# Products of keys and queries for the transposed scores as 64-row tiles, two banks at a time

## The reference, cut to what matters

```python
B, T, D, S, H = 32, 112, 256, 375, 16            # DH = 16
def xattn(k, q):                                 # k = context (B, S, D), q = layernorm(x) (B, T, D)
    qh, kh, vh = heads(q @ wq + bq), heads(k @ wk + bk), heads(k @ wv + bv)
    logits = einsum('bhqd,bhkd->bhqk', qh, kh) / sqrt(16) + mask * -1e9
    return einsum('bhqk,bhkd->bhqd', softmax(logits), vh) @ wo + bo
x = x + xattn(ctx, layernorm(x))
x = x + moe_ffn(layernorm(x))                    # top-1 of 8 experts, 1024 hidden units
```

## Time and profile before

| | us |
|---|---|
| median of 3 runs | 864.75 |
| lowest, highest | 863.34, 866.98 |
| profiled execution, its own time | 873.9 |
| its span, first to last instruction | 872.2 |

### The profile page before, as it was taken

How to read it: one execution, slowest core, us unless ns; L and a number is a source line. 1 busy time by engine, 2 the same in 40 slices (tenths; PEclk the granted TensorE clock), 3 DMA queues, 4 the chain that set the end, 5 groups by cost and what they waited for, 6 DMA issues and landing times.

```text
span 872.2 us, 27918 instructions
## 1 busy us (share of the span) xinstructions
PE 781.0 (90%) x8480; PEld 554.7 (64%) x8480; DVE 565.9 (65%) x1823; ACT 435.5 (50%) x1032; POOL 523.5 (60%) x753
## 2 busy tenths in 40 slices
PE   5799999999999999999999999981698988987894
PEld 4466666666666666666666666550577867776683
DVE  4667777777777777777777777638354545554352
ACT  3266666666666666666666666540323323322231
POOL 5676677677766777777677677561535435445311
PEclk9899999999999999999999999995799999999798
DMA  5776577667766876788678767605312222222110
GB/s 164 201 182 187 162 199 202 184 170 198 208 166 181 198 218 182 205 211 226 167 209 217 209 186 191 176 13 214 109 47 80 65 62 80 63 66 86 39 31 8
DMA packets 103239, 129.94 MB, mean 149 GB/s; under 512 B 12973, under 2 KB 89799, under 8 KB 102664
## 3 DMA queue, kind: packets, MB, share of 16 engines
q1 hardware_dynamic: 96744, 115.98, 49.5%
q0 software_dynamic: 5600, 12.87, 4.8%
q10 hardware_dynamic: 832, 0.27, 0.2%
HBM read 93.94 MB, written 36.06 MB: 149 GB/s over the span
## 4 chain that ended last, share of the span: by engine, by line
PE 88%; issue 5%; DVE 3%; DMA 1%; ACT 1%; ACTq 0%; POOL 0%; POOLq 0%; DVEq 0%
PE ps L1474 12%; PE ps L1454 11%; PE ps L1244 10%; PE ps L1209 10%; PE ps L1203 9%; PE ps L1260 8%; PE ps L1274 8%; PE ps L1183 5%; PE ps L1295 4%; PE ps L1323 4%; PE ps L1309 2%; PE ps L1298 1%; PE ps L1439 1%; PE ps L1194 1%; PE ps L1316 1%
## 5 line engine op out<-in xcount | busy, mean ns | idle before, releaser
L912 ACT ACTIVATE arena_b<-ps 128x448 f32<-128x448 f32 (+1 forms) x384 | 193.9, 540 | 120.4 <-PE ps L1203 87.7
L1643 DVE CUSTOM_DVE_ANT_0 arena_w<-ps,arena_w 112x375 bf16<-112x375 f32 x256 | 140.3, 548 | 78.6 <-PE ps L1183 73.8
L1070 ACT ACTIVATE arena_b<-ps,b_sb 128x256 f32<-128x256 f32 (+1 forms) x168 | 61.8, 439 | 164.0 <-PE ps L1454 103.6
L1643 DVE CUSTOM_DVE_ANT_0 arena_b<-ps,arena_w 112x375 bf16<-112x375 f32 x256 | 139.9, 546 | 0.0
L1209 PE MATMUL ps<-arena_b,arena_w 128*128 128x448 bf16 x384 | 131.6, 357 | 0.4 <-DVE arena_b L1654 0.4
L1203 PE MATMUL ps<-arena_b 128*128 128x224 f16 x768 | 131.9, 260 | 0.0
L1474 PE MATMUL ps<-arena_w,arena_b 128*128 x840 | 108.8, 284 | 24.7 <-issue 23.6
L1474 PEld LDWEIGHTS ps<-arena_w,arena_b 128*128 128x128 f16 x840 | 83.9, 101 | 46.2 <-issue 33.5
L1454 PE MATMUL ps<-arena_b,w_parts 128*128 128x256 f16 (+1 forms) x1008 | 107.2, 258 | 3.3 <-issue 3.2
L833 POOL DMA_INDIRECT arena_b<-rows,arena_b x35 | 37.3, 1066 | 108.1 <-DVE arena_b L1885 85.3
L1866 DVE TENSOR_SCALAR arena_b<-arena_b 128x512 f16<-128x512 f32 x70 | 31.1, 445 | 107.0 <-ACT arena_b L1070 88.5
(11 more groups left out here) (204 smaller groups left out, 1290.6 us busy)
## 6 DMA issues: line engine op xcount, KB each, us to landing
arena_b<-k_spill SPq DMA_DIRECT2D x128, 192.0 KB, 3.9
arena_b<-in_L_ffn_W SPq DMA_DIRECT2D x64, 256.0 KB, 4.6
arena_b<-q_spill SPq DMA_DIRECT2D x128, 112.0 KB, 4.3
k_spill<-arena_b SPq DMA_DIRECT2D x32, 384.0 KB, 2.5
arena_b<-in_ctx SPq DMA_DIRECT2D x32, 375.0 KB, 5.0
arena_w<-in_x SPq DMA_DIRECT2D x64, 112.0 KB, 4.7
q_spill<-arena_w SPq DMA_DIRECT2D x32, 224.0 KB, 2.1
rows<-arena_w SPq DMA_DIRECT2D x32, 224.0 KB, 2.3
```

The costliest lines, as they stand in the source:

```text
L912: nc.scalar.activation(probsT[u % PROB_BUFFERS][0:n], scoreT_bank[c][0:n, 0:QUAD * T], ACT.Exp, scale=1.0 / SCALE_SCORES).then_inc(probs_r ...
L1070: last = nc.scalar.activation(h_act[g % H_BANKS][:, i * n:(i + 1) * n], ps[:, 1 + g % H_BANKS, i * n:(i + 1) * n], ACT.Silu, bias=b1_sb[:, ...
L1643: nc.vector.tensor_tensor_reduce(out=masked_scores[r % 2], in0=shared_bank[r][0:T, 0:S], in1=mask_bias, scale=-1.0, scalar=3.4e38, op0=ALU ...
```

## The change

- In `scores_transposed` the work goes by pairs of units (2p and 2p+1), which lie in two different banks. Each head's product is its own: 64 rows and 112 columns. The stacked rows are laid out anew: first heads of all pairs in rows 0 to 63, second heads in rows 64 to 127. The masked copy of the queries is not needed in the product, and `q_stack` is half as large.
- A pair of units is: two maxima products (224 columns now, for first heads of the one unit and second heads of the other), four head products (`first_heads`: the first heads of one unit alternate with the second heads of the other, so the two row tiles write to different banks), two more maxima products, a wait of the PE for its own `first_heads` (`heads_written`), and the other four head products with the roles of the banks exchanged. For pair 0 the head products come first, before the wait for the maxima.
- The units' places in the PE's order move: pair 1 (units 2, 3) stands where unit 2 stood, pair 2 (4, 5) where units 4 and 5 did, pair 3 (6, 7) where unit 6 did, pair 4 (8, 9) where units 7 and 8 did, pair 5 (10, 11) where units 10 and 11 did.
- Keys and queries are stacked by eight transfers each instead of four, of 16 partitions each; a row of queries is 448 bytes instead of 896. The spilled queries have their parts in another order.
- `values` reads the exponentials of a quad in the order of heads that results (`place_of`). Three semaphores of the opening are merged into others.

```diff
-        Q_MOVED, K_MOVED = 16 * len(GROUPS), 16 * len(GROUPS)
+        Q_MOVED, K_MOVED = 2 * 16 * len(GROUPS), 2 * 16 * len(GROUPS)
...
-                    for g, (part, _) in enumerate(GROUPS):
-                        sp.dma_start(k_stack[par][32 * g:32 * g + 32].rearrange("p r j k -> p r (j k)"),
-                                     k_spill[par][part].rearrange("(r i) n -> i r n", r=PAIRS)
-                                     ).then_inc(k_stacked[par], 16)
+                    for a in range(2):
+                        for g, (part, _) in enumerate(GROUPS):
+                            sp.dma_start(k_stack[par][stack_rows(a, g)].rearrange("p r j k -> p r (j k)"),
+                                         k_spill[par][part].rearrange("(r a d) n -> a d r n", r=PAIRS, a=2)[a]
+                                         ).then_inc(k_stacked[par], 16)
...
-                def products(c, start):
-                    j = quad // 2
+                def head(u, i, a, start=False, stop=False):
+                    quad, c = u // CHUNKS, u % CHUNKS
+                    j, r = quad // 2, (2 * quad + i) % PAIRS
+                    rows, first = slice(P // 2 * a, P // 2 * (a + 1)), (2 * a + i) * T
+                    return pe.matmul(scoreT_bank[c][:, first:first + T], k_stack[par][rows, r, j, c * P:(c + 1) * P],
+                                     q_stack[par][rows, r, j, :], start=start, stop=stop)
+
+                def first_heads(start):
                     for i in range(2):
-                        r = (2 * quad + i) % PAIRS
-                        mm = pe.matmul(scoreT_bank[c][:, 2 * i * T:2 * (i + 1) * T], k_stack[par][:, r, j, c * P:(c + 1) * P],
-                                       q_stack[par][:, r, j].rearrange("p a t -> p (a t)"), start=start and i == 0,
-                                       stop=not start and i == 1)
-                    return mm
+                        head(units[0], i, 0, start=start and i == 0)
+                        mm = head(units[1], i, 1, start=start and i == 0)
+                    mm.then_inc(heads_written, 1)
...
                 else:
-                    for c in chunks:
-                        wait_count(pe, probs_ready, UNITS * b + CHUNKS * quad + c - (CHUNKS - 1))
-                        maxima_and_mask(c, True)
-                        products(c, False).then_inc(scoresT_ready, 1)
+                    bank_read(units[0])
+                    maxima_and_mask(units[0], 0, True)
+                    bank_read(units[1])
+                    maxima_and_mask(units[1], 1, True)
+                    first_heads(False)
+                maxima_and_mask(units[0], 1)
+                maxima_and_mask(units[1], 0)
+
+                pe.wait_ge(heads_written, PAIRS_OF_UNITS * b + pair + 1)
+                head(units[0], 0, 1)
+                head(units[1], 0, 0)
+                head(units[0], 1, 1, stop=True).then_inc(scoresT_ready, 1)
+                head(units[1], 1, 0, stop=True).then_inc(scoresT_ready, 1)
...
                 if st.exists(1):
-                    scores_transposed(st, 0, (2,))
+                    scores_transposed(st, 1)
...
-                if st.exists(1):
-                    scores_transposed(st, 3, (0,))
...
                 if st.exists(1):
-                    scores_transposed(st, 3, (1, 2))
+                    scores_transposed(st, 5)
```

More of the change, by code:

```diff
@@ L410, in build @@
         k_spilled = sem("k_spilled")
+        heads_written = sem("heads_written")
         q_stacked = [sem("q_stacked0"), sem("q_stacked1")]
@@ L492, in _, with stack_rows @@
         def _(sp):
+            def stack_rows(a, g):
+                first = 4 * DH * a + DH * g
+                return slice(first, first + DH)
             def load_batch(b, parity):
@@ L524, in step @@
                     wait_apart(sp, k_spilled, 16 * (b + 1), sp_passed)
-                    for g, (part, _) in enumerate(GROUPS):
-                        sp.dma_start(k_stack[par][32 * g:32 * g + 32].rearrange("p r j k -> p r (j k)"),
-                                     k_spill[par][part].rearrange("(r i) n -> i r n", r=PAIRS)
-                                     ).then_inc(k_stacked[par], 16)
-                    wait_apart(sp, q_spilled, 16 * (b + 1), sp_passed)
[L530 to L533, removed]
+                    for a in range(2):
[3 more added lines that the diff above has]
+                                         ).then_inc(k_stacked[par], 16)
+                    wait_apart(sp, q_spilled, 16 * (b + 1), sp_passed)
+                    for a in range(2):
+                        for g, (_, part) in enumerate(GROUPS):
+                            sp.dma_start(q_stack[par][stack_rows(a, g)].rearrange("p r j t -> p r (j t)"),
+                                         q_spill[par][part, :, a * DT * T:(a + 1) * DT * T].rearrange(
+                                             "(r a d) n -> a d r n", r=PAIRS, a=2)[a]
+                                         ).then_inc(q_stacked[par], 16)
                 if st.exists(-1) and st.exists(-3):
@@ L670, in mask_queries @@
                 wait_count(pool, scores_ready, QUADS * (b - 1) if st.in_loop or b > 1 else 0)
-                rows = pair_keep.unsqueeze(1).to_broadcast([P, DT, 2, T])
+                rows = pair_keep.unsqueeze(2).to_broadcast([P, 2, DT, T])
                 for part in range(2):
                     pool.wait_ge(q_low_ready if part else q_high_ready, DT * (b + 1))
-                    pool.tensor_tensor(q_parts[par][:, part], q_split[:, part].unsqueeze(2).to_broadcast([P, DT, 2, T]),
+                    pool.tensor_tensor(q_parts[par][:, part], q_split[:, part].unsqueeze(1).to_broadcast([P, 2, DT, T]),
                                        rows, ALU.mult).then_inc(q_parts_ready, 1)
@@ L1194, in transpose_maxima, with place_of, scores_transposed, maxima_and_mask @@
                 pe.transpose(max_bank[:, 0:T], maxima, ident[0:T, 0:T]).then_inc(maxT_ready, 1)
-            def scores_transposed(st, quad, chunks):
+            def place_of(r):
+                return 2 * (r % 2) + r // 2
+            def scores_transposed(st, pair):
                 b, par = st.batch(1), st.parity(1)
-                def products(c, start):
-                    j = quad // 2
-                    for i in range(2):
-                        r = (2 * quad + i) % PAIRS
-                        mm = pe.matmul(scoreT_bank[c][:, 2 * i * T:2 * (i + 1) * T], k_stack[par][:, r, j, c * P:(c + 1) * P],
-                                       q_stack[par][:, r, j].rearrange("p a t -> p (a t)"), start=start and i == 0,
-                                       stop=not start and i == 1)
-                    return mm
[L1208 to L1212, removed]
+                units = (2 * pair, 2 * pair + 1)
+                def head(u, i, a, start=False, stop=False):
[4 more added lines that the diff above has]
+                                     q_stack[par][rows, r, j, :], start=start, stop=stop)
+                def maxima_and_mask(u, a, start=False):
+                    quad, c = u // CHUNKS, u % CHUNKS
+                    return pe.matmul(scoreT_bank[c][:, 2 * a * T:2 * (a + 1) * T], mask_keys[:, quad, c, :],
+                                     max_rows[par].rearrange("p (i a) t -> p a i t", a=2)[:, a], start=start, stop=False)
+                def bank_read(u):
+                    wait_count(pe, probs_ready, UNITS * b + u - (CHUNKS - 1))
+                def first_heads(start):
+                    for i in range(2):
+                        head(units[0], i, 0, start=start and i == 0)
+                        mm = head(units[1], i, 1, start=start and i == 0)
+                    mm.then_inc(heads_written, 1)
+                if pair == 0:
```

50 lines of the change are left out of this document (23 added, 27 removed).

## The result

| | before | after |
|---|---|---|
| median, us | 865.87 (863.34 to 870.92) | 911.23 (909.47 to 914.02) |
| ratio, 95% interval | | 1.0519 (1.0463 to 1.0576) |
| span of the profiled execution, us | 872.2 | 910.0 |
| a step, mean of 24 (the sixth to the twenty-ninth), us | 17.215 | 18.638 |

The changed kernel is 45 us slower; 43 were forecast. The step is the better measure: it is read within one profiled execution, from the first product of scores 0 in one step to that in a later one. 24 steps of the changed kernel lie between the first and the last of these rows of the PE's timeline (start us, length us, what); 1.42 us more a step in 32 steps is 45.5 us.

A forecast was written before the change was run, and what follows sets the result against it. The PE, busy 90% of the span, was taken to bound the kernel, with some starts set by DVE. The stretches summed to 1.34 us a step, 43 us in 32 steps, added to the median 864.75: 908 us, range 867 to 930.

The forecast's parts named there:

- Tiles run together, changes of tiling cost: In each pair, two row tiles stream together, 0.58 us for 0.76; entering tiles costs 0.09, leaving 0.14; pair 1.04.
- Rival 1: Changes between 128 and 64 rows are free: +0.02 us a step, 865 to 869 us; chance 0.13.
- Stretches after scores 1, 2, 3: Pairs 2, 4 and 5 outgrow DVE's wait: 1.35 us against 1.19, 1.18 and 1.19; +0.16, +0.17, +0.16 a step.
- Pair 3: Replaces unit 6 and the change to L1244: 0.99 us for 0.47, +0.52 a step.
- Unit 9 gives nothing back: Its 0.38 us leaves the place before values 2, but scores 3 waits for DVE's chain from project_queries: 0.
- Scores 1 behind ACT's copy: Unit 3 leaves the place before scores 1, which then waits for ACT's copy of the values: +0.05 us a step.
- Pair 0 costs nothing: After scores 0 the pair takes 1.21 us, within the 1.27 that DVE sets: nothing.
- The wait for heads_written costs nothing here: Signal comes 0.3 us after the last first head started; maxima products and the change back to tiles cover it: nothing.
- SP's eight more issues cost nothing: Eight more issues take 3.6 us and delay the x rows; POOL's cover of 1.9 us before scores 0 absorbs it: nothing.
- Rival 4: POOL or SP becomes late: L674 missing scores 0 by 1 us a step adds 32 us, 940 us; chance 0.03.
- pairs 1 and 3: Pair 1 replaces units 2 and 3, +0.28 us a step; pair 3 replaces unit 6 and a tiling change, +0.52.

The follow-up runs named there:

- full_height_x_first: Changed kernel with each head's product over all 128 stacked rows and the x rows' load issued ahead of the stacking: 18.005 us a step, ratio 1.0285.
- unit9_early: Kernel before with unit 9 alone moved up, right behind units 7 and 8, in front of project_queries: 17.409 us a step, ratio 1.0077.
- order_only: Kernel before with the units at the places they have after the change, products unchanged: 17.713 us a step, ratio 1.0178.
- x_rows_first: Changed kernel with the load of the x rows issued ahead of the stacking instead of behind it: 18.591 us a step, ratio 1.0530.
- eight_transfers: Kernel before with stacked keys and queries read by eight transfers each, halves of 16 partitions: 18.940 us a step, ratio 1.0606.
- full_height_heads: Changed kernel with each head's product over all 128 stacked rows, its order, wait and eight transfers kept: 18.494 us a step, ratio 1.0448.
- full_height_no_wait: full_height_heads with the PE's wait for heads_written deleted: 18.259 us a step, ratio 1.0397.

## Why the prediction was right, and where it was not

- **Tiles run together, changes of tiling cost.** Right. Entering measured 0.10 to 0.11 (0.09 forecast); leaving 0.095, not the 0.14 of the 32-row tiles. A pair up to the next full-height product is 0.99 to 1.01 for the 1.04 forecast. Rival 1 (free changes) falls with full_height_x_first: heads at full height would then have been slower than tiles.
- **Stretches after scores 1, 2, 3.** 1.31 each for the 1.35 forecast, from 1.19 to 1.20: together 0.35 more a step where 0.49 was forecast. The price of leaving the tiles was too high there.
- **Pair 3.** 369.23 to 370.22, 0.99, as forecast.
- **Unit 9 gives nothing back.** Right, 373.54 to 375.74 is 2.20; unit9_early shows it alone. Without this step the forecast would have been 12 us lower.
- **Scores 1 behind ACT's copy.** The place was right, the size not: `values` 0 to scores 1 is 0.81 (365.29 to 366.10) against 0.70, +0.11 for +0.05. order_only, which has the products of before, takes the same 0.82, so the cause is the place of the units, not the tiles. The copy ends at 365.77, 0.33 before scores 1, where I had taken 0.27:

```profile
365.39 0.38 ACT L958 ACTIVATE arena_b<-ps 128x256 f32<-128x256 f32 x1 [0.69 <-PE ps L1301]
```

- **Pair 0 costs nothing.** Wrong. Scores 0 to `project_keys` takes 1.56 us in every other step where it was 1.36 to 1.39 before, and 1.33 in the others for 1.27: +0.13. (Two of the 24 steps have 2.18 and 1.90, which is the ring; in x_rows_first they have 1.56 and 1.33 too.) Timeline of the kernel before, behind scores 0 at 403.10, then of the changed kernel:

```profile
403.48 0.56 PE L1203 MATMUL ps<-arena_b 128*128 128x224 f16 x4
403.87 0.54 PE L1209 MATMUL ps<-arena_b,arena_w 128*128 128x448 bf16 x2
```

```profile
341.73 0.37 PE L1189 MATMUL ps<-arena_b,arena_w 32*112 32x375 f16 x4
342.07 0.27 PE L1213 MATMUL ps<-arena_b 64*128 64x112 f16 x4
342.59 0.56 PE L1218 MATMUL ps<-arena_b,arena_w 128*128 128x224 bf16 x4 [0.25 <-DVE arena_b L1677]
```

  The maxima products wait for DVE's spreading of the maxima (L1677). Before, four products of 224 columns stood in front of them, 0.39 of stream; now four heads of 0.10 in all, and the other four heads stand behind the wait. I had added up the stream and not asked what the shortened part used to cover. The rows show the wait; no run changes it alone.
- **The wait for heads_written costs nothing here.** Right. PE's loads wait for it for 29.7 us in total, yet the heads start 0.19 after the last maxima product's start, with the wait in front of them and without it (191 to 192 ns both times): the change of tiling covers it. Uncovered it costs 0.165 a step.
- **SP's eight more issues cost nothing.** The reason was wrong. I took 1.9 us between the masked queries and scores 0 as cover. But the x rows wait on SP behind q_spill, and q_spill on the masked queries: what is late in one step is later in the next, until the ring sets the step. Rival 4 had the place, with 0.03 of chance, and the wrong reason to dismiss it. In a kernel with nothing else changed it costs 51 us, more than all the PE's terms. That the changed kernel loses only some 5 us by it was luck: I had not compared the ring's round with the step.

How could the sum still be right? First, by errors that cancel. Pair 0 and scores 1 cost 0.19 a step more than forecast, the three stretches after scores 1, 2 and 3 cost 0.14 less, and `transpose_attention`, which I left out, is 0.02 shorter; pairs 1 and 3 and unit 9 came as forecast. That makes 1.38 for 1.34, which is the PE's path with the ring open (18.591 - 17.215). That it is so close is in part luck.

Second, because a step takes the longer of two bounds, not their sum, and in the changed kernel the PE's is the longer. The ring is late at first and then catches up. Two of its rounds are in these rows of SP's timeline; the rows below them, from the timelines of the PE and of POOL, show scores 0 late at the start of the first round, and the masked queries and scores 0 again 220 us further on:

```profile
137.41 0.37 SPq L577 DMA_DIRECT2D q_spill<-arena_w  x1
...
155.27 0.37 SPq L577 DMA_DIRECT2D q_spill<-arena_w  x1
...
173.32 0.37 SPq L577 DMA_DIRECT2D q_spill<-arena_w  x1
```

```profile
136.84 0.37 PE L1189 MATMUL ps<-arena_b,arena_w 32*112 32x375 f16 x4 [0.54 <-POOL arena_w L680]
```

```profile
355.65 2.05 POOL L680 TENSOR_TENSOR arena_w<-arena_w 128x448 f16<-128x448 f16 x2 [0.55 <-ACT arena_w L943]
```

```profile
360.76 0.37 PE L1189 MATMUL ps<-arena_b,arena_w 32*112 32x375 f16 x4 [0.56 <-issue]
```

These rounds and the two that follow take 18.1 us in the mean, half a microsecond less than the PE's 18.6, and so the ring gains on the PE step by step. From the eleventh step on the masked queries are complete 1.9 to 3.1 us before scores 0, as in the kernel before (2.3 to 2.9), and at 355.65 the masking waits for ACT's queries. Such waits are 0.3 us a step in the mean there, so the ring itself would then need 18.3. In eight_transfers (18.94), full_height_heads (18.49) and full_height_no_wait (18.26) the ring is the longer bound, since the PE's own step there is 17.2 to 18.0.

The rounds of the four kernels differ by one part. From the issue of the x rows' load to POOL's residual it takes 4.5 us in the mean of eight_transfers, 4.0 in full_height_heads, 3.8 in full_height_no_wait, 3.5 in the four rounds above; the rest is 14.4 to 14.6 in all. The shorter rows of the queries can't be the whole reason, since the first three all read 896 bytes a row. What sets that time was not tried.

The path of 1.42 us, part by part as the runs give it: places 0.50, split products at full height 0.13, the wait 0.165, tiles instead of full height 0.59, the ring 0.05 (all of it before the eleventh step). The 0.59 is what the changes of tiling cost less the stream that tiles save and the wait that they cover. The shares hold for this order of undoing: the wait costs 0.165 at full height and nothing between tiles.

## What to carry to other kernels

Price a change of tiling like an instruction: here some 0.1 us each way, so a group of tiles had to save more than 0.2 us of stream before it paid, and four 64-row heads saved some 0.09 (0.20 from the first to the work behind them at full height, 0.11 of stream in tiles). Before counting a queue's extra work as covered, follow it round: if what it delays is what the queue waits for a step later, compare the whole round with the step, not the slack of one pass; here the cure was the place of one load. And where an expected loss is found in full, undo it in parts all the same: here errors of both signs cancelled, and a second bound lay 0.3 to 0.5 us under the first, ready to take over.

## What the runs showed of the hardware that was not expected

- Leaving 64-row tiles for full height took 95 ns after the stream, leaving 32-row tiles 138 ns (294 from start to start with 156 of stream), both in the changed kernel.
- Splitting a transfer in two halves of 16 partitions doubled SP's time for it: eight issues of half size take 3.63 us, four of full size 1.78; an issue costs some 0.45 us in both.

```profile
341.12 3.63 SPq L530 DMA_DIRECT2D arena_b<-k_spill  x8
344.88 3.62 SPq L536 DMA_DIRECT2D arena_b<-q_spill  x8
```
